# A hybrid attention, delta-rule and feed-forward layer on one Trainium2 core: where the chunks of a serial scan stand in VectorE's program

## What is computed

```
x = x + attention(ln(x))    # 32 heads of 8, keys of the own and the previous 128 tokens
x = x + ffn(ln(x))          # 4-bit weights with LoRA, 256 -> 1024 -> 256, relu
x = x + block_b(ln(x))      # below
x = x + ffn(ln(x))          # the same weights again
```

```
err = S k_t - v_t
S   = S - beta_t * err * k_t^T
o_t = S q_t
```

## Time and profile before

| | |
|---|---|
| three runs | 1322.96, 1328.42, 1329.11 us; median 1328.42 us |
| the profiled execution | 1326.07 us; its span 1324.2 us; mean granted TensorE clock 0.885 |
| busy share of the span | PE 81%, DVE 71%, ACT 38%, POOL 13% |
| chain that ended last | PE 42%, DVE 37%, ACT 9% |
| body 0 | 199.5 to 328.7 us: 129.2 us |
| bodies 1 to 5 | 147.3, 144.0, 146.3, 144.0 and 146.2 us |
| bodies 6 and 7 with what is behind them | 125.5 and 142.0 us |

### The profile page before, as it was taken

How to read it: one execution, slowest core, us unless ns; L and a number is a source line. 1 busy time by engine, 2 the same in 40 slices (tenths; PEclk the granted TensorE clock), 3 DMA queues, 4 the chain that set the end, 5 groups by cost and what they waited for, 6 DMA issues and landing times.

```text
span 1324.2 us, 22011 instructions
## 1 busy us (share of the span) xinstructions
PE 1076.3 (81%) x8600; PEld 729.6 (55%) x8600; DVE 946.2 (71%) x2425; ACT 497.4 (38%) x1027; POOL 172.2 (13%) x251
## 2 busy tenths in 40 slices
PE   4698869687979997989878997899798987940787
PEld 2355635364556754766466654675476645730565
DVE  3823278877886788867985788868986689679611
ACT  2043254136422643355422642354333533520132
POOL 2000000401040014000130004000310104003100
PEclk9589879788878998999978998999988988985788
DMA  9633024113310232004301231014200300020000
GB/s 295 119 60 55 16 69 88 20 33 83 74 20 24 61 93 38 11 24 107 66 10 32 73 78 35 25 33 108 52 2 25 91 1 1 17 72 0 16 8 8
DMA packets 93607, 67.69 MB, mean 51 GB/s; under 512 B 47232, under 2 KB 86336, under 8 KB 93504
## 3 DMA queue, kind: packets, MB, share of 16 engines
q1 hardware_dynamic: 88544, 60.75, 19.3%
q10 hardware_dynamic: 4960, 5.54, 1.5%
HBM read 45.55 MB, written 20.32 MB: 50 GB/s over the span
## 4 chain that ended last, share of the span: by engine, by line
PE 42%; DVE 37%; ACT 9%; SPq 4%; DMA 3%; issue 3%; POOL 1%; ACTq 0%; DVEq 0%; POOLq 0%
DVE lane_buf L1182 6%; PE bank L1441 6%; PE bank L1694 6%; DVE state L1201 5%; PE bank L1621 5%; DVE u_l L1189 5%; DVE state L1194 4%; PE bank L1703 4%; DVE mx L998 4%; PE bank L1646 3%; PE bank L1500 3%; PE bank L1549 3%; PE bank L1717 2%; PE bank L1421 2%; DVE hid L1151 2%
## 5 line engine op out<-in xcount | busy, mean ns | idle before, releaser
L697 ACT ACTIVATE probs<-bank 128x512 f32<-128x512 f32 x256 | 152.1, 597 | 216.4 <-PE bank L1534 216.1
L1549 PE MATMUL bank<-probs,v_ext 128*9 128x128 f32 x2048 | 164.0, 281 | 14.0 <-ACT probs L697 8.5
L998 DVE TENSOR_REDUCE mx<-bank 128x2 f32<-128x320 f32 x256 | 120.9, 484 | 45.9 <-PE bank L1500 40.9
L1694 PE MATMUL bank<-feat_c,wgu 128*128 128x256 f32 (+1 forms) x384 | 96.3, 404 | 56.6 <-DVE hid_c L1249 50.9
L1495 PE MATMUL bank<-edge_mask,identb 128*128 128x64 bf16 x512 | 64.9, 213 | 86.0 <-DVE mx L998 73.7
L339 POOL TENSOR_TENSOR lane_buf<-state,q_l 128x128 f32<-128x128 f32 x128 | 83.8, 684 | 291.6 <-DVEq L1207 291.6
L1549 PEld LDWEIGHTS bank<-probs,v_ext 128*9 128x9 f32 x2048 | 84.0, 91 | 58.4 <-issue 21.8
L1182 DVE TENSOR_TENSOR lane_buf<-state,til 128x128 f32<-128x128 f32 x256 | 103.0, 402 | 18.1 <-POOL lane_buf L584 10.2
L1694 PEld LDWEIGHTS bank<-feat_c,wgu 128*128 128x128 f32 (+1 forms) x384 | 71.5, 192 | 77.4 <-DVE hid_c L1249 54.6
L1495 PEld LDWEIGHTS bank<-edge_mask,identb 128*128 128x128 bf16 x512 | 34.1, 104 | 141.6 <-DVE mx L998 98.7
L1529 PE MATMUL bank<-tri_mask,identb 128*128 128x512 bf16 x256 | 103.4, 404 | 0.5 <-DMA q_stack<-m_rows 0.5
(11 more groups left out here) (167 smaller groups left out, 1766.8 us busy)
## 6 DMA issues: line engine op xcount, KB each, us to landing
k_pieces<-conv SPq DMA_DIRECT2D x48, 128.0 KB, 2.3
k_stack<-k_pieces SPq DMA_DIRECT2D x32, 192.0 KB
k_stack<-k_pieces SPq DMA_DIRECT2D x32, 128.0 KB
k_l<-lane_k SPq DMA_DIRECT2D x8, 512.0 KB, 3.6
q_l<-lane_q SPq DMA_DIRECT2D x8, 512.0 KB, 5.6
q_pieces<-conv SPq DMA_DIRECT2D x24, 128.0 KB, 2.0
q_stack<-q_pieces SPq DMA_DIRECT2D x32, 96.0 KB
tok<-in_x SPq DMA_DIRECT2D x8, 256.0 KB, 2.8
```

The lines of the kernel that those rows point to most:

```text
L697: act.activation(probs[:, u % 2], score_bank[u % 2][:], ACT.Exp, scale=float(DK) ** -0.5).then_inc(exp_done, 1)
L998: dve.tensor_reduce(mx[:, g, 2 * v:2 * v + 2], bank[1 + u % 2][:, 0:2 * SPAN].rearrange("p (h k) -> p h k", h=2), AX.X, ALU.max).then_inc( ...
L1549: last = pe.matmul(bank[5][row:row + VE, col:col + W], v_ext[:, b, kb, h, :], probs[:, u % 2, (hp * 2 + kb) * W:(hp * 2 + kb + 1) * W], st ...
L1694: last = pe.matmul(late_bank[i % 2][0:m, g * BT:(g + 1) * BT], wgu[:, k, g * INTER + 128 * i:g * INTER + 128 * i + m], fc[:, k], start=(k ...
```

## The change

Slots are no longer four to each step. A step without maxima keeps four; a step of 14 to 17 has two, one for each of its maxima; the steps 25 to 32 have two and three in turn (25 has two, 26 three). That is 80 slots, so 20 chunks beside attention instead of 25. Three chunks (20 to 22) stand before `first_residual` and one (23) before `first_apply`, as many as before; the other eight stand in pairs behind the gated tiles 0, 1, 2 and 3. Tile 4 follows `first_sums`, tile 5 the first two pieces of `second_terms`. `second_sums` moves from before `second_residual` to behind the eight maxima that follow it.

```
-                MAX_AT[4 * (step - BEGIN) + 1 + 2 * at] = (dn, v + (0 if dn else DONE_EARLY * UPG))
-        PIECES_AT = {4 * (18 - BEGIN) + k: (0, 3, k) for k in range(4)}
-        OUT_AT = {4 * (step - BEGIN) + 2: g for g, step in enumerate((11, 19, 27))}
-        CUTS = N_UNITS + 1 - BEGIN, 28, 29, NC_
+        SLOT_AT = [0]
+        for step in range(BEGIN, N_UNITS + 1):
+            n_slots = 4
+            if step in PASS1:
+                n_slots = 3 - step % 2 if PASS1[step][0] else 2
+            SLOT_AT.append(SLOT_AT[-1] + n_slots)
+                MAX_AT[SLOT_AT[step - BEGIN] + at] = (dn, v + (0 if dn else DONE_EARLY * UPG))
+        PIECES_AT = {SLOT_AT[18 - BEGIN] + k: (0, 3, k) for k in range(4)}
+        OUT_AT = {SLOT_AT[step - BEGIN] + 1: g for g, step in enumerate((11, 19, 27))}
+        CUTS = SLOT_AT[-1] // 4, 23, 24
+        LATE_CUTS = 24, 26, 28, 30, NC_
...
-                if tail:
-                    act_of(s, 0)
-                if has_scan:
-                    scan(t, CUTS[2], CUTS[3], False, False)
-                if tail:
-                    act_of(s, 1)
+                for i in range(4):
+                    if tail:
+                        act_of(s, i)
+                    if has_scan:
+                        scan(t, LATE_CUTS[i], LATE_CUTS[i + 1], False, False)
                 if has_scan:
                     step = first_sums(t)
                 if tail:
-                    act_of(s, 2)
-                for i in range(C):
-                    if has_scan:
-                        step = second_terms(i, step)
-                    if tail and 3 + i < IT:
-                        act_of(s, 3 + i)
+                    act_of(s, 4)
                 if has_scan:
-                    second_sums(step)
+                    step = second_terms(0, step)
+                    step = second_terms(1, step)
+                if tail:
+                    act_of(s, 5)
+                if has_scan:
+                    step = second_terms(2, step)
+                    step = second_terms(3, step)
                 if following:
                     second_residual(n)
...
                     max_pieces(n + 1, 2)
+                if has_scan:
+                    second_sums(step)
                 if tail:
                     third_residual(s)
```

## The result

| | before | after |
|---|---|---|
| median of 4 runs | 1326.97 us (1322.96 to 1329.11) | 1280.23 us (1277.41 to 1284.56) |
| the profiled execution; its span | 1326.07; 1324.2 us | 1278.25; 1276.4 us |
| mean granted TensorE clock | 0.885 | 0.908 |
| bodies 0 to 7 | as in the table of the profile before | 127.5, 137.3, 136.9, 136.8, 136.6, 136.6, 123.1, 140.6 |

The ratio is 0.9649, 95% interval [0.9613, 0.9685], so 46.7 us or 3.5% faster; 1283.7 us was forecast, in a range of 1266 to 1304. By the profiled executions the kernel won 47.8 us where the sum had 42.4.

What follows compares the result with a forecast made beforehand. VectorE was taken to bound attention and TensorE the feed-forward; 6.7 us in each of bodies 1 to 5, plus 3.8, 3.4 and 1.7 in bodies 0, 6 and 7, made 42.4 off 1326.1: 1283.7 us, range 1266 to 1304.

Steps and rivals of the forecast that it cites:

- The bound by stage: VectorE holds the stage beside attention, TensorE the feed-forward; the change moves work from the one to the other's gaps.
- Attention, 6.4: Scan beside attention ends 7.2 us sooner at full clock, 5.5 if the 0.81 clock dip returns; the middle was taken.
- rival 1: TensorE's clock stays up in attention and behind it, 1.8 us more per body over seven bodies: 1271 us, chance 0.20.
- GpSimd's terms: Small steps behind attention regain 1.2 us; ten chunks lose 1.1 us, first residual's norm and first apply 0.8.
- rival 2: GpSimd's terms hold VectorE back in the feed-forward, one block of 3 to 4 us per chunk in all: 1302 us, chance 0.17.
- rival 3: Both two-input products of every chunk are blocked by GpSimd, VectorE losing 9.2 us instead of 1.1: 1340 us, chance 0.03.
- End of the scan to tile 0, 0 with 1.6 at most from the clock: From scan's end to the first gated tile: no net change, at most 1.6 us from clock against 0.8 of blocks.
- Feed-forward, -0.9: VectorE gets 5.0 us more work against its idle time, so the second residual comes 0.9 us late.
- Behind the second residual, 0: The second sum, 3.35 us, fits VectorE's 5.90 us gap before the third residual; its outputs keep 2 to 3 us spare.
- rival 5: Late output transfers hold ScalarE's squares and what follows, by 2 to 3 us per body: 1300 us, chance 0.05.
- Body 0, 3.8: Body 0 gains only 3.8 us, having no gated tiles and only 1.24 us of idle time.
- Body 6, 3.4: Body 6 gains 3.4 us: no maxima follow its second residual, and late outputs find ScalarE waiting, 1.5 us by estimate.

Runs made afterwards that it cites:

- run 7: The kernel before with 30 extra matmuls per body on TensorE, ahead of the maxima it waits for at the end of attention: 1318.57 us, ratio 0.9943.
- run 2: The changed kernel with four slots in every step again, so 25 chunks beside attention, tiles and second sum as changed: 1318.45 us, ratio 0.9933.
- run 6: The kernel before without GpSimd's terms of the first 16 chunks, a copy of one column in their place: 1309.01 us, ratio 0.9868.
- run 10: The kernel before with GpSimd's first terms begun after chunk 25 instead of after chunk 21: 1319.31 us, ratio 0.9929.
- run 4: The changed kernel with 22 chunks beside attention instead of 20, and six behind the tiles: 1314.87 us, ratio 0.9905.

## Why the prediction was right

**The bound by stage** held. TensorE ends the stretch beside attention now (the waits of 0.59 and 0.32, and 18 chunks winning 0.3 us only), and VectorE took the chunks in the gap ahead of the second residual. The total is nearer than its terms: in body 2 the 1.2 us too few behind the scan and the 1.4 too many ahead of tile 0 cancel, and 7 us of the odd bodies that the sum does not have stand against 3.1 that bodies 0 and 6 fell short and 1.45 of a later start. That much of the agreement is luck.

**Attention, 6.4:** 7.1 us in each steady body. The walk from step to step gave 7.2 at full clock, and the clock stayed full at the place of the 0.81. Taking the middle with the returned dip was a term that was mis-sized, by 0.7: this half of rival 1 was right. VectorE's small steps of 0.17 us at 503.71 stand 0.1 us from the walk, counted from the scan's start.

**GpSimd's terms:** the 1.2 us of the first group are 1.4, by 0.72 instead of 2.11 us. Before, four products of chunks beside attention had been held up too (0.47, 0.62, 0.78 and 0.58 us, and a gap of 0.50), 1.7 us that my account of the terms left out; they are inside the 7.1, which TensorE's bound caps. The 0.8 us around the first residual are 1.65 (0.44 and 0.2 us on two products, 1.0 on the first apply). Eight chunks and four tiles, 520.72 to 534.50, took 13.8 instead of 12.8, but the terms end at 527.90 and so lie beside only four of these chunks, which lost 0.4 us (one product of 0.75); another 0.5 was lost at 527.91, beside the GpSimd addition that follows the terms. Two first products of chunks among the tiles, 0.75 and 0.84 us, are the prediction's sign of rival 2, but only two of eight. So rival 3 was far off, and rival 2 too, but blocks on single instructions are dearer than I took them.

The Trainium skill (SBUF — State Buffer, section "SBUF: two separate sides") has GpSimd and VectorE, where its instruction has two inputs in SBUF or runs in a two-port mode, lock each other out for a whole instruction. By that rule, as the prediction estimates, ten chunks would have lost about 7 us. The trace agrees for instructions that stand alone (a first apply of 1.75 instead of 0.74, small steps of 0.58 instead of 0.17), and not for chunks: the six beside the terms (22 to 27) lost 1.1 us together, in three of their twelve products.

**End of the scan to tile 0, 0 with 1.6 at most from the clock.** The low clock of the kernel before held tile 0 back by 1.9 us in body 2 (run 7), more than the 1.6 that I had as the most. In the changed kernel it is 0.57 again in body 2, and yet the way from the scan's end to tile 0 became 1.0 us shorter (18.00 to 17.01): 1.4 by the small steps, 1.0 by shorter waits for TensorE, and 1.4 back on blocked instructions. The two halves that I set against each other were of the right sign, and the one on blocks was the larger.

**Feed-forward, -0.9:** -0.4. The residual is 0.5 us behind the down product.

**Behind the second residual, 0:** -0.5 in body 2. TensorE waits 2.08 us for VectorE at 547.54 and its clock is 0.75 in the stretch, so the down product ends later. The sum itself is hidden, and its outputs come in time in bodies 1 to 6 and 0.27 us late in body 0, so rival 5 did not occur.

**The odd bodies** are the largest error: 2.2 to 2.6 us each, three times. I took body 2 for all five. The others were longer in the table of the profile before, 147.3, 146.3 and 146.2 us against 144.0, with a clock of 0.68 and 0.76 at two places. The first no longer counts: from chunk 20 to tile 0 all five bodies take 9.9 us, whatever their clock. The second is not gone: between the second and the third residual the clock of the changed kernel is 0.75 to 0.76 in bodies 1 to 3, body 2 among them, and 0.87 in bodies 4 and 5. Why the bodies alternated before is not shown; that they stopped in runs 2, 6, 7 and 10 too says that it took little.

**Body 0, 3.8:** 1.7. VectorE waits 1.45 and 1.12 us for two maxima at 215.50 and 217.92, where TensorE's clock was 0.53 for 3.4 us, so attention gave 4.9 instead of 6.4; behind the second residual 1.4 more were lost, with the second sum there. **Body 6, 3.4:** 2.4, but not as told: 4.3 us were won up to tile 0 instead of 6.4, 0.7 was lost at the third residual and 1.2 behind it. ScalarE did not wait for outputs; TensorE's clock was 0.76 from 1093 to 1100. **Body 7, 1.7:** 1.7, from 142.3 us before (the table of the profile before has 142.0). The scan of body 0 starts 1.45 us later. In run 10, whose program ahead of it is that of the kernel before, it starts 2.5 us later, so such a difference comes without a change.

Five bodies of 8.7, 1.7, 2.4 and 1.7, less 1.45, are 47.8.

## What to carry to other kernels

Work moved to an engine's gap is worth what it weighs only while the other engine can follow, and the two were found by a walk over single steps, not by busy shares. When the gap is full, the next thing in it must go too: half the gain hung on the sum's new place. And a signal that releases another engine moves with the work: a count of 22 instead of 21 chunks put GpSimd's terms over the small steps and cost 26 us until the signal was moved alone.

Of a pipeline, read more than one body before multiplying, and before calling what an edit won the price of what it removed: in runs 2, 6, 7 and 10 more than half of the gain lay in the three odd bodies.

## What the runs showed of the hardware

The granted clock was not the same for the same part of the program. In the changed kernel the stretch from 38.0 to 40.7 of a body has TensorE busy for 1.58 to 1.59 of 2.70 us in all five steady bodies. What follows, in bodies 1, 2 and 4:

```profile
369.10:377.10 8.00, 6.91 (x67) 4.82 (x64) 6.95 (x22) 2.63 (x8) 1.46 (x3) 1.00 0.12 16
...
780.10:788.10 8.00, 7.31 (x63) 5.01 (x61) 6.03 (x19) 2.33 (x7) 0.39 (x1) 0.80 0.10 13
```

Body 2 has 0.57 there (the row above). From the scan's end to tile 0 bodies 1, 2 and 4 took 16.2, 17.0 and 17.3 us: where the clock fell it cost about 1 us, and no more at 0.57 (17.0) than at 0.80 (17.3). Most of the stretch lies beside VectorE's work.

A VectorE instruction that was blocked by GpSimd lost much the same whatever its length: a small step 0.41 us (0.17 to 0.58), a product of chunk 22 0.44 (0.38 to 0.82), each half of the first apply about 0.5. So the tiny ones suffer most for their size. In run 4 all eight small steps beside the terms were blocked (0.58 to 0.91 us), in the changed kernel only three of the twelve products of chunks 22 to 27.
